# Four places for the split projections, the shared expert moved to the start, and the last stage's loads moved ahead, in a two-layer attention and expert kernel

## The chip, the cores and the metric

The kernel runs on one core of one Trainium2 chip. What counts is the device time of the whole program in microseconds (us), as the median of several runs. The core has five engines that run their own instruction lists and wait for each other by semaphores: PE (TensorE, matmul), DVE (VectorE), ACT (ScalarE), POOL (GpSimd) and SP (SyncE, which here only issues DMAs).

## What is computed

The input x has 4096 tokens of 128 features (2 sequences of 2048). Cut to what matters here, the reference is:

```
xn = layernorm(x)
s  = attention_block(xn)              # 8 heads on 64 features, and 8 heads on their Holt-smoothed copy
g  = silu(moe(xn))                    # 32 experts, 4 of them per token, plus a shared expert
x  = x + s * g
xn = layernorm(x); s = selective_scan_block(xn); g = silu(routed_mlp(xn)); x = x + s * g

# in moe:
scores = softmax(xn @ wg.T); keep the 4 best of 8 groups; top 4 experts; rank of each token in its expert
y = sum over the 4 experts of w * (silu(xe @ w1) * (xe @ w3)) @ w2
z = silu(xf @ sw1) * (xf @ sw3) @ sw2          # the shared expert, on all 4096 tokens
return y + z
```

## The kernel before

The order of all work is written out by hand, engine by engine; `wait_ge(sem, n)`, `after(engine, sem, n)` and, on SP, `hold(sem, n)` are the waits. Each engine's list runs in order, so a wait holds back all that stands behind it. Tokens are taken in `NB` = 8 blocks of 512. The program's stages are:

1. **Start.** Normalisation and its transpose `XNT` (L1514), routing logits (L1520), the Holt level (L1526 to L1534), with the attention input `XC`, which lies in the tile `YM`. `XC` is also stored to DRAM as `xct_d` (L473).
2. **Projections and routing.** For each block j PE makes Q and K (`qk`, L1564, two banks of PSUM, in turn 4, 5 and 6, 7) and V (`values`, L1572). Q and K go to DRAM as three bf16 parts each, whose sum is the float32 value: ACT writes the leading part (`lead`, L1166), DVE the remainder (`remainder`, L677), ACT the middle part (`middle`, L1172), POOL the last part (`part2`, L1432), and SP stores all six to `ql_d` and `kl_d` (L437). The parts of a block have one of two places, `part(parts, level, j % 2)`. DVE has the `remainder` calls written between the routing's top-4 search (L712 to L718), which ends in `sel_done` (L721). Then PE sums the selection over tokens (`ranks`, L1553 and L1554, in banks 0 to 3), and DVE makes each token's rank in its expert out of it (L730 to L752).
3. **Attention.** 16 units (8 groups of heads for 2 sequences). A unit's Q and K come back by 12 DMAs into `stacks` (L449, L451). DVE takes row maxima of the scores (`unit_max`, L758) out of PSUM banks 4 to 7, a unit ahead of the exponentials on ACT (L1202); PE does scores for the maxima (L1588), scores (L1633) and weighed values (L1606). In the second half of the units POOL scatters the tokens to their experts (L1472).
4. **Experts.** 32 experts, each a transpose, two products, a product back, and a store of the result to `oe_d` (L521).
5. **Shared expert.** PE (L1705, L1706), ACT (L1247), DVE (L804), PE (L1698), DVE (L797, into `YM`), over the 8 blocks, with the weights of "expert 32".
6. **Tail of layer 0 and projections of layer 1.** SP writes the softmax sums' reciprocals to DRAM (L525), loads the attention results of blocks 0 and 1 (`load_attn`, L533 to L535), and the constants of layer 1 (L554 to L556). DVE starts with a wait for all of these constants, then `normalise` (L830, L831), `attn_stats` (L813), `attn_apply` (L824 to L844), and `combine(j)` (L862), which adds to `YM` the four expert outputs of each token, gathered by POOL with 16 indirect DMAs to a block (L1497). The gathers start when all stores of L521 have landed.
7. **Selective scan and the last MLP** of layer 1.

## Time and profile before

| | us |
|---|---|
| median of 3 runs | 2137.68 (2133.76 to 2138.3) |
| the profiled execution, its time | 2140.73 |
| its span | 2138.9 |
| PE busy | 1884.9 |
| DVE busy | 1776.4 |
| ACT busy | 1444.4 |
| POOL busy | 344.0 |

The profile has one execution. PE is busy for 88% of the span and DVE for 83%, but both are averages over stages with different limits, so a change in one stage is read from that stage: which engine or DMA ends its waits.

### The profile page before, as it was taken

How to read it: one execution, taken by the hardware profiler on the slowest of the kernel's cores; microseconds unless marked ns; L12 is line 12 of the kernel's file. 1: busy time of each engine (PE TensorE's matmuls, PEld its weight loads, DVE VectorE, ACT ScalarE, POOL GpSimd, SP SyncE). 2: the span in 40 equal slices, each digit the busy share in tenths (PEclk: the TensorE clock that was granted, in tenths of full speed). 3: DMA queues.
4: the chain of work that ended last, by engine and by line, in shares of the span. 5: the costliest groups of instructions: out<-in, count | busy, mean ns of one | idle time of the engine just before them, and what ended most of it. 6: DMA issues, size and time to landing. Idle time of an engine off the chain costs nothing.

```text
span 2138.9 us, 33478 instructions
## 1 busy us (share of the span) xinstructions
PE 1884.9 (88%) x11734; PEld 719.9 (34%) x11734; DVE 1776.4 (83%) x2689; ACT 1444.4 (68%) x2807; POOL 344.0 (16%) x516
## 2 busy tenths in 40 slices
PE   7537999999999999999999999988997887599884
PEld 6201222222222222222222222216764444266563
DVE  6689999999999999999999999903347887478778
ACT  5204888888888888888888888883322344567542
POOL 1210000000000222222222222000027652000000
PEclk9656999999999999999999999999998889799896
DMA  3231121120010111111111111016754332321321
GB/s 84 83 116 44 46 71 65 47 84 26 25 35 24 40 46 36 46 42 35 51 38 38 49 37 49 8 32 178 205 162 123 108 112 73 101 71 54 101 76 30
DMA packets 145888, 144.01 MB, mean 67 GB/s; under 512 B 29451, under 2 KB 124687, under 8 KB 145572
## 3 DMA queue, kind: packets, MB, share of 16 engines
q1 hardware_dynamic: 137380, 124.71, 19.2%
q0 software_dynamic: 8352, 17.29, 2.7%
q8 instruction: 89, 1.46, 0.3%
q14 instruction: 67, 0.55, 0.1%
HBM read 81.06 MB, written 60.03 MB: 66 GB/s over the span
## 4 chain that ended last, share of the span: by engine, by line
PE 70%; DVE 14%; ACT 8%; issue 3%; DMA 2%; SPq 2%; POOL 1%; DVEq 0%; ACTq 0%
PE PS L1606 23%; PE PS L1633 18%; PE PS L1588 8%; DVE mxp L758 6%; PE PS L1680 3%; ACT probs L1202 3%; ACT SG L1187 2%; PE PS L1736 2%; PE PS L1836 2%; PE PS L1854 1%; PE PS L1667 1%; PE PS L1745 1%; PE PS L1857 1%; PE PS L1839 1%; DMA xs_d<-SG 1%
## 5 line engine op out<-in xcount | busy, mean ns | idle before, releaser
L758 DVE TENSOR_REDUCE mxp<-PS 128x1 f32<-128x1024 f32 x1024 | 1203.5, 1220 | 43.9 <-PE PS L1588 29.2
L1202 ACT ACTIVATE probs<-PS 128x512 f32<-128x512 f32 x2048 | 1061.7, 604 | 168.1 <-PE PS L1633 164.9
L1633 PE MATMUL PS<-stacks 51*128 51x512 bf16 x2048 | 615.8, 383 | 28.2 <-ACT probs L1202 16.8
L1588 PE MATMUL PS<-stacks 48*128 48x512 bf16 x2048 | 518.9, 393 | 49.1 <-DVE mxp L758 30.4
L1606 PE MATMUL PS<-probs,VH 128*32 128x512 f32 x4096 | 546.7, 606 | 6.8 <-ACT SG L1187 6.1
L1633 PEld LDWEIGHTS PS<-stacks 51*128 51x128 bf16 x2048 | 154.3, 94 | 681.1 <-ACT probs L1202 611.7
L1588 PEld LDWEIGHTS PS<-stacks 48*128 48x128 bf16 x2048 | 109.5, 94 | 217.0 <-DVE mxp L758 178.0
L1472 POOL DMA_INDIRECT xe_d<-xn_s,rows_s x128 | 126.0, 984 | 328.5 <-PE PS L1606 292.6
L1497 POOL DMA_INDIRECT VP<-oe_d,ROWI x128 | 133.4, 1042 | 255.7 <-DMA oe_d<-stacks 194.7
L771 DVE TENSOR_TENSOR stacks<-stacks,PS 128x640 f32<-128x640 f32 x32 | 26.2, 820 | 134.7 <-ACT stacks L1234 134.7
L1606 PEld LDWEIGHTS PS<-probs,VH 128*32 128x32 f32 x4096 | 81.6, 108 | 125.0 <-issue 109.2
L1450 POOL CAST spl<-nmx 128x16 bf16<-128x16 f32 x32 | 6.3, 196 | 562.8 <-DVE nmx L761 476.5
L1680 PE MATMUL PS<-stacks,ews 128*128 128x320 f32 x256 | 76.4, 441 | 5.9 <-DVE stacks L771 4.1
L1736 PE MATMUL PS<-wa,wff 128*128 128x512 f32 x64 | 47.1, 902 | 26.1 <-ACT wa L1257 26.1
L1234 ACT ACTIVATE stacks<-PS 128x640 f32<-128x640 f32 x32 | 22.5, 704 | 59.7 <-PE PS L1680 59.7
L1680 PEld LDWEIGHTS PS<-stacks,ews 128*128 128x128 f32 x256 | 46.1, 190 | 27.3 <-issue 9.0
L1191 ACT ACTIVATE mT<-PS 48x128 bf16<-48x128 bf16 x32 | 8.5, 267 | 67.2 <-PE PS L1594 67.2
L1458 POOL TENSOR_TENSOR VH<-VP,bvb 128x128 f32<-128x128 f32 x32 | 14.3, 451 | 202.1 <-PE PS L1606 202.1
L1260 ACT ACTIVATE probs<-PS,bcol 128x512 f32<-128x512 f32 x32 | 22.0, 687 | 31.4 <-PE PS L1736 31.4
L1225 ACT ACTIVATE stacks<-PS 128x640 f32<-128x640 f32 x32 | 22.5, 703 | 30.2 <-PE PS L1659 30.2
L1667 PEld LDWEIGHTS PS<-ews,stacks 128*128 128x128 f32 x320 | 40.7, 192 | 6.5 <-DVE stacks L771 1.6
L1564 PE MATMUL PS<-YM,wsq 128*128 128x512 f32 x32 | 24.7, 916 | 20.2 <-DVE wa L677 20.2
(344 smaller groups left out, 1922.4 us busy)
## 6 DMA issues: line engine op xcount, KB each, us to landing
xe_d<-zt SPq DMA_DIRECT2D x16, 640.0 KB
stacks<-xe_d SPq DMA_DIRECT2D x32, 320.0 KB, 3.3
oe_d<-stacks SPq DMA_DIRECT2D x32, 320.0 KB, 2.4
o_d<-SG SPq DMA_DIRECT2D x256, 32.0 KB, 1.6
ews<-in_ew_dram SPq DMA_DIRECT2D x33, 192.0 KB, 2.3
stacks<-ql_d SPq DMA_DIRECT2D x64, 96.0 KB
stacks<-kl_d SPq DMA_DIRECT2D x64, 96.0 KB
probs<-xs_d SPq DMA_DIRECT2D x18, 256.0 KB, 3.7
```

The source lines that it names most:

```text
L758: v.tensor_reduce(mxp[:, n // 2, n % 2:n % 2 + 1], MXB[n % 2].rearrange("p a c -> p (a c)"), X_AX, ALU.max).then_inc(mx_done, 1)
L1187: act.activation(OE[half][:, :], OB, ACT.Copy).then_inc(o_evac, 1)
L1202: act.activation(probs[:, at:at + 512], PS[:, bank_of(u, e), :], ACT.Exp, scale=float(1.0 / np.sqrt(np.float32(DK)))).then_inc(exp_done, 1)
L1472: pool.indirect_dma_start(xe_d, bass.IndirectOffsetOnAxis(rows_s[i][:, n:n + 1], 0), xn_s[i][:, :], None, bounds_check=E * CAP - 1, oob_is ...
L1497: pool.indirect_dma_start(GB[:, t % (2 * TB), n, :], None, oe_d, bass.IndirectOffsetOnAxis(ROWI[:, t, n:n + 1], 0), bounds_check=E * CAP, ...
L1588: mm = pe.matmul(MXB[n % 2][:, i, :], QS[w][o:o + MAXROWS, (n // 2) * P:(n // 2 + 1) * P], KS[w][o:o + MAXROWS, key:key + 512], start=True ...
L1606: mm = pe.matmul(OB[32 * jg:32 * jg + 32, :], VH[w][:, kt, :], probs[:, at:at + 512], start=(kt < 2), stop=(kt >= TCH - 2))
L1633: pe.matmul(PS[:, bank_of(u, e), :], KS[w][o:o + KROWS + 3, kt * P:(kt + 1) * P], QS[w][o:o + KROWS + 3, q0:q0 + 512], start=True, stop=Tr ...
L1667: mm = pe.matmul(o, hhe[w % 2][:, t * P:(t + 1) * P], EW[w][:, 2, :], start=True, stop=True)
L1680: mm = pe.matmul(PS[:, 2 + 2 * m + h, 0:CAP // 2], EW[w][:, m, :], xeT[w % 2][:, h * CAP // 2:(h + 1) * CAP // 2], start=True, stop=True)
L1736: pe.matmul(PS[:, 2 + f % 2, :], wff1[:, f * P:(f + 1) * P], f_(wa[3]), start=True, stop=True).then_inc(f_ready, 1)
L1836: pe.matmul(PS[:, b, :], BELOW, scaled[:, b, :], start=True, stop=True)
```

## The change

It has three parts.

- **Four places for the parts.** Blocks j % 4 of 0 and 1 keep the two places of before, blocks 2 and 3 get places in `stacks` (`QS[1]` to `QS[3]`, which are empty until the first unit loads). ACT's `lead(j)` waits for the store of block j-4 where it waited for that of block j-2.
- **The shared expert at the start.** It is taken out from behind the experts, on PE, ACT and DVE. Its weights are loaded behind x. On PE `shared_in(0)` stands ahead of `ranks`, the rest of it behind, ahead of the first scores for the maxima. ACT now takes the silu (into `SHG`) and also copies the other product out (`SHV`), POOL multiplies the two (`SHH`), and ACT copies the result to `YM`: DVE has no instruction of it. `SHG`, `SHV` and `SHH` lie in the tiles of the experts' weights, of `affine` and of `wff`, so the loads of `affine` and `wff` come later. `xct_d` is stored before the parts, since `YM` gets its result early. A `sem_inc(sums_read)` on DVE tells PE that banks 2 and 3 are read.
- **The tail's loads earlier.** `wff`, `affine` and all constants of layer 1 but `win` are loaded at the start of the attention; the reciprocal sums are stored at expert 8; `load_attn(0)` is issued at expert 30, ahead of the last two stores. Behind the last store come `load_attn(1)` and `win`.

```diff
@@ SP
+            load_weights(sp, E)
             for dst, src in CONSTS0:
...
-            sp.dma_start(affine[:, :, :], a["affine"].partition_broadcast(P)).then_inc(c_ld, 16)
             hold(ones_set, 5)
...
+            hold(h_out, TCH // TB)
+            hold(xc_ready, NB)
+            sp.dma_start(xct_d, XC).then_inc(xct_st, 16)
             for j in range(NB):
                 hold(part2, j + 1)
                 for parts, src, stored in ((ql_d, QPARTS, ql_st), (kl_d, KPARTS, kl_st)):
                     hold(stored, 48 * j)
                     for lv in range(3):
-                        sp.dma_start(parts[lv, :, j * 512:(j + 1) * 512], part(src, lv, j % 2)).then_inc(stored, 16)
+                        sp.dma_start(parts[lv, :, j * 512:(j + 1) * 512], part(src, lv, j % 4)).then_inc(stored, 16)
...
+            hold(c_ld, 16 * NCONST)
+            hold(sh_out, NB)
+            for dst, src in CONSTS_LATE:
+                sp.dma_start(dst, a[src]).then_inc(c_ld, 16)
+            sp.dma_start(affine[:, :, :], a["affine"].partition_broadcast(P)).then_inc(c_ld, 16)
+            sp.dma_start(alog[:, 0:2, :], a["alog"].partition_broadcast(P)).then_inc(c_ld, 16)
+            sp.dma_start(sc_aff[:, :, :], a["sc_aff"].partition_broadcast(P)).then_inc(c_ld, 16)
             repeat(sp, GROUPS // 4, lambda k: group(k, clear=True))
...
+                if e == 8:
+                    hold(at_sum, 1)
+                    for j in range(NB):
+                        sp.dma_start(rl_d[:, j * 512:(j + 1) * 512], LS[0][G * j:G * j + G, :]).then_inc(rl_st, 16)
+                if e == E - 2:
+                    hold(rl_st, 16 * NB)
+                    hold(xct_st, 16)
+                    hold(xt_ready, E)
+                    load_attn(0)
...
+            hold(hh_done, E)
             load_attn(1)
-            for dst, src in CONSTS1:
-                sp.dma_start(dst, a[src]).then_inc(c_ld, 16)
-            sp.dma_start(alog[:, 0:2, :], a["alog"].partition_broadcast(P)).then_inc(c_ld, 16)
-            sp.dma_start(sc_aff[:, :, :], a["sc_aff"].partition_broadcast(P)).then_inc(c_ld, 16)
+            hold(c_ld, 16 * NLATE)
+            sp.dma_start(win[:, :], a["win"]).then_inc(c_ld, 16)
@@ ACT
-                after(act, ql_st, 48 * (j - 1))
-                after(act, kl_st, 48 * (j - 1))
+                after(act, ql_st, 48 * (j - 3))
+                after(act, kl_st, 48 * (j - 3))
...
+            act.wait_ge(xct_st, 16)
+            for j in range(NB + 1):
+                if j < NB:
+                    act.wait_ge(sh_ready, j + 1)
+                    after(act, sh_product, j - 1)
+                    act.activation(SHG[j % 2], PS[:, 4 + 2 * (j % 2), :], ACT.Silu)
+                    act.activation(SHV[j % 2], PS[:, 5 + 2 * (j % 2), :], ACT.Copy).then_inc(sh_gated, 1)
+                if j > 0:
+                    act.wait_ge(sh_projected, j)
+                    act.activation(YM[:, TB * (j - 1):TB * j, :], PS[:, 2 + (j - 1) % 2, :].rearrange("p (t d) -> p t d", d=D), ACT.Copy).then_inc(sh_out, 1)
             write_rows(0, 1)
@@ POOL
+            for j in range(NB):
+                pool.wait_ge(sh_gated, j + 1)
+                after(pool, sh_projected, j - 1)
+                pool.tensor_tensor(SHH[j % 2], SHG[j % 2], SHV[j % 2], ALU.mult).then_inc(sh_product, 1)
@@ PE
+            def shared_in(j):
+                after(pe, sh_gated, j - 1)
+                for n in range(2):
+                    mm = pe.matmul(PS[:, 4 + 2 * (j % 2) + n, :], EW[0][:, n, :], XNT[:, j * 512:(j + 1) * 512], start=True, stop=True)
+                mm.then_inc(sh_ready, 1)
+
+            def shared_project(j):
+                pe.wait_ge(sh_product, j + 1)
+                after(pe, sh_out, j - 1)
+                for t in range(TB):
+                    mm = pe.matmul(PS[:, 2 + j % 2, t * P:(t + 1) * P], SHH[j % 2][:, t * P:(t + 1) * P], EW[0][:, 2, :], start=True, stop=True)
+                mm.then_inc(sh_projected, 1)
+
+            pe.wait_ge(ew_ld[0], 16)
+            pe.wait_ge(rest, NB - 1)
+            shared_in(0)
             pe.wait_ge(v_out, NB)
             ranks()
+            pe.wait_ge(rest, NB)
+            shared_in(1)
+            pe.wait_ge(sums_read, 1)
+            for j in range(NB):
+                shared_project(j)
+                if j + 2 < NB:
+                    shared_in(j + 2)
```

On PE, between the projections and the attention, there stood only the four products of `ranks`, and then the scores for the maxima:

```order
40 L1553 MATMUL PS<-probs,cst 128x512
41 L1554 MATMUL PS<-probs,onesq 128x512
42 L1553 MATMUL PS<-probs,cst 128x512
43 L1554 MATMUL PS<-probs,onesq 128x512
44 L1588 MATMUL PS<-stacks 128x512 x72
```

Now it is this (L1592 is `shared_in`, L1599 `shared_project`; four pairs of the same rows follow before the last two shown):

```order
40 L1592 MATMUL PS<-XNT,ews 128x512 x2
41 L1564 MATMUL PS<-probs,cst 128x512
42 L1565 MATMUL PS<-probs,onesq 128x512
43 L1564 MATMUL PS<-probs,cst 128x512
44 L1565 MATMUL PS<-probs,onesq 128x512
45 L1592 MATMUL PS<-XNT,ews 128x512 x2
46 L1599 MATMUL PS<-ews,wff 128x128 x4
47 L1592 MATMUL PS<-XNT,ews 128x512 x2
...
58 L1599 MATMUL PS<-ews,wff 128x128 x8
59 L1622 MATMUL PS<-stacks 128x512 x72
```

The scores for the maxima, 44 before and 59 now, have all eight blocks of the shared expert ahead of them.

On SP, behind the experts' last stores, there stood:

```order
473 L521 DMA oe_d<-stacks 128x5x128 x4
474 L525 DMA rl_d<-probs 16x512 x8
475 L533 DMA stacks<-o_d 128x1x512 x2
476 L534 DMA stacks<-rl_d 128x1x512
477 L535 DMA stacks<-xct_d 128x512
478 L533 DMA stacks<-o_d 128x1x512 x2
479 L534 DMA stacks<-rl_d 128x1x512
480 L535 DMA stacks<-xct_d 128x512
481 L554 DMA stacks<-in_win_dram 128x644
...
487 L556 DMA sc_aff<-in_sc_aff_dram 128x768
```

Now there stands (L535 to L537 is `load_attn`, L569 the experts' store):

```order
471 L569 DMA oe_d<-stacks 128x5x128 x3
472 L535 DMA stacks<-o_d 128x1x512 x2
473 L536 DMA stacks<-rl_d 128x1x512
474 L537 DMA stacks<-xct_d 128x512
475 L569 DMA oe_d<-stacks 128x5x128 x2
476 L535 DMA stacks<-o_d 128x1x512 x2
477 L536 DMA stacks<-rl_d 128x1x512
478 L537 DMA stacks<-xct_d 128x512
479 L574 DMA stacks<-in_win_dram 128x644
```

One `load_attn` has moved ahead of the last two stores, the stores of L525 have moved up to expert 8, and of the constants only `win` is left behind `load_attn(1)`.

## Rows read from the trace of the kernel before

**Rows 1.** Windows: us; busy PE, PEld, DVE, ACT, POOL; PE clock, DMA share, GB/s

```profile
98.00:111.00 13.00, 0.62 (x3) 0.33 (x2) 7.37 (x8) 5.20 (x10) 2.29 (x3) 0.63 0.22 74
...
300.00:600.00 300.00, 291.81 (x1972) 69.33 (x1964) 289.20 (x252) 260.74 (x513) 9.42 (x36) 1.00 0.16 51
...
1585.00:1607.00 22.00, 21.41 (x99) 13.28 (x97) 10.60 (x17) 6.06 (x9) 13.05 (x14) 1.00 0.77 206
```

**Rows 2.** The chain of waits, one round of the projections: start, us, what

```profile
99.48 0.69 ACT HH L1166
...
106.47 2.01 DMA kl_d<-wa
108.59 0.69 ACT HH L1166
```

**Rows 3.** Groups of DVE, 61.5 to 107.2 us: busy, mean ns, idle before

```profile
L677 DVE SCALAR_TENSOR_TENSOR wa<-PS,bcol,HH 128x512 f32<-128x512 f32 x5 | 3.8, 751 | 17.5 <-ACT SG L1166 17.5
...
L713 DVE TENSOR_TENSOR probs<-probs,WK 128x1024 bf16<-128x1024 f32 x2 | 3.6, 1804 | 0.1
```

**Rows 4.** Timeline of DVE: start, us, instruction, idle before it

```profile
55.30 2.06 DVE L718 SCALAR_TENSOR_TENSOR probs<-probs 128x1024 f32<-128x1024 bf16 x1
...
59.97 1.23 DVE L713 TENSOR_TENSOR probs<-probs,WK 128x1024 bf16<-128x1024 f32 x1
...
106.50 0.69 DVE L721 TENSOR_SCALAR probs<-probs 128x1024 f32<-128x1024 f32 x1
...
117.37 1.22 DVE L730 COPY probs<-PS 128x1024 f32<-128x1024 f32 x1 [3.98 <-PE PS L1554]
...
139.84 36.29 DVE L758 TENSOR_REDUCE mxp<-PS 128x1 f32<-128x1024 f32 x32
```

**Rows 5.** Timeline of POOL in the projections

```profile
54.15 2.13 POOL L1432 TENSOR_TENSOR SG<-wa,HH 128x512 bf16<-128x512 f32 x1 [25.44 <-ACT wa L1172]
...
101.86 1.15 POOL L1432 TENSOR_TENSOR SG<-wa,HH 128x512 bf16<-128x512 f32 x1 [6.96 <-ACT wa L1172]
```

**Rows 6.** Timeline of PE, projections to the first maxima

```profile
48.21 1.88 PE L1564 MATMUL PS<-YM,wsq 128*128 128x512 f32 x4
...
93.16 3.75 PE L1564 MATMUL PS<-YM,wsq 128*128 128x512 f32 x4 [4.09 <-DVE wa L677]
96.71 1.92 PE L1572 MATMUL PS<-wsq,YM 128*128 128x128 f32 x8
111.43 2.07 PE L1553 MATMUL PS<-probs,cst 128*128 128x512 f32 x2 [12.81 <-ACT VP L1180]
...
135.94 1.04 PE L1588 MATMUL PS<-stacks 48*128 48x512 bf16 x4 [18.67 <-DMA stacks<-kl_d]
```

**Rows 7.** Timeline of PE, one block of the shared expert

```profile
1593.83 1.05 PE L1698 MATMUL PS<-ews,HH 128*128 128x128 f32 x8
...
1596.44 1.05 PE L1698 MATMUL PS<-ews,HH 128*128 128x128 f32 x8
```

**Rows 8.** The chain of waits, experts to tail

```profile
1600.30 7.42 DMA sc_aff<-in_sc_aff_dram
1607.74 0.70 DVE stacks L830
```

**Rows 9.** Timeline of SP: first load of unit 0; L525's stores behind the experts

```profile
121.72 0.80 SPq L449 DMA_DIRECT2D stacks<-ql_d  x1
...
1586.60 3.82 SPq L525 DMA_DIRECT2D rl_d<-probs  x8
```

**Rows 10.** Timeline of POOL and DVE: gathers of two blocks, and their use

```profile
1589.99 1.05 POOL L1497 DMA_INDIRECT VP<-oe_d,ROWI  x1 [194.67 <-DMA oe_d<-stacks]
...
1630.98 1.14 POOL L1497 DMA_INDIRECT VP<-oe_d,ROWI  x1 [0.30 <-issue]
...
1627.75 4.66 DVE L862 SCALAR_TENSOR_TENSOR YM<-VP,WK,YM 128x128 f32<-128x128 f32 x16
...
1649.10 4.66 DVE L862 SCALAR_TENSOR_TENSOR YM<-VP,WK,YM 128x128 f32<-128x128 f32 x16
```

More of the change, by code:

```diff
@@ L287, in build @@
         ones_set = sem("ones_set")
-        x_ld = [sem(f"x_ld{i}") for i in range(NB // 2)]
+        xz_ld = [sem(f"xz_ld{i}") for i in range(4)]
         var_ready, std_ready = sem("var_ready"), sem("std_ready")
@@ L339, in build @@
                              "g_st"))
-        z_ld, fw_ld = [sem(f"z_ld{i}") for i in range(4)], sem("fw_ld")
+        fw_ld = sem("fw_ld")
+        sh_ready, sh_gated, sh_product, sh_projected, sh_out, sums_read = (
+            sem(n) for n in ("sh_ready", "sh_gated", "sh_product", "sh_projected", "sh_out", "sums_read"))
         yl_ready, pr_ready, s2_done = (
@@ L367, in build @@
                                               wa[0].rearrange("p t c -> p (t c)"), wa[3].rearrange("p t c -> p (t c)"))]
+        ews_flat = ews.rearrange("p e m c -> p (e m c)")
+        aff_flat = affine.rearrange("p i c -> p (i c)")
+        SHG = [ews_flat[:, 3 * P + i * 512:3 * P + (i + 1) * 512] for i in range(2)]
+        SHV = [aff_flat[:, i * 512:(i + 1) * 512] for i in range(2)]
+        SHH = [wff[:, i * 512:(i + 1) * 512] for i in range(2)]
         QPARTS, KPARTS = halves16[0:3], halves16[3:6]
@@ L467, in load_max @@
                     sp.dma_start(QS[w][o + KROWS:o + KROWS + 3, :], mT[:, :]).then_inc(m_ld[w], 16)
-            hold(h_out, TCH // TB)
-            hold(xc_ready, NB)
-            sp.dma_start(xct_d, XC).then_inc(xct_st, 16)
             load_max(0, 0)
@@ L623, in _ @@
                 for i in range(GP):
-                    hold(z_ld[i], 32 * s)
+                    hold(xz_ld[i], 32 * s + 16)
                     if s >= 2:
@@ L676, in remainder @@
                 for n, (left, parts) in enumerate(((QREST, QPARTS), (KREST, KPARTS))):
-                    ins = v.scalar_tensor_tensor(left[w], PS[:, 4 + 2 * w + n, :], bcol[:, n:n + 1], part(parts, 0, w), ALU.add, ALU.subtract)
+                    ins = v.scalar_tensor_tensor(left[w], PS[:, 4 + 2 * w + n, :], bcol[:, n:n + 1], part(parts, 0, j % 4), ALU.add, ALU.subtract)
                 ins.then_inc(rest, 1)
@@ L790, in _ @@
             expert_out(E - 1, 3, E // 2 - 1)
-            def shared_out(j, w):
-                v.wait_ge(mo_ready, E + j + 1)
-                if isinstance(j, int) and j == 0:
-                    v.wait_ge(xct_st, 16)
-                v.tensor_copy(YM[:, bass.ds(TB * j, TB), :], PS[:, 4 + w, :].rearrange("p (t d) -> p t d", d=D)).then_inc(ym_done, 1)
-            def shared(k):
-                for w in range(2):
-                    j = 2 * k + w
-                    v.wait_ge(sg_done, E + j + 1)
-                    after(v, mo_ready, E + j - 1)
-                    v.tensor_tensor(HH[w][:, :], SG[w][:, :], PS[:, 2 + w, :], ALU.mult).then_inc(hh_done, 1)
-                    if not (w == 0 and isinstance(k, int)):
-                        shared_out(j - 1, 1 - w)
-            repeat(v, NB // 2, shared)
-            shared_out(NB - 1, 1)
+            v.wait_ge(c_ld, 16 * NLATE)
             def stats(src, groups, bn, agg):
@@ L1171, in middle @@
                 for left, parts in ((QREST, QPARTS), (KREST, KPARTS)):
-                    ins = act.activation(part(parts, 1, j % 2), left[j % 2], ACT.Copy)
+                    ins = act.activation(part(parts, 1, j % 4), left[j % 2], ACT.Copy)
                 ins.then_inc(part1, 1)
@@ L1241, in _ @@
                 act.wait_ge(oe_st[half], 64 * UNITS)
-            def shared(k):
-                for w in range(2):
-                    act.wait_ge(mh_ready, E + 2 * k + w + 1)
-                    act.wait_ge(hh_done, E + 2 * k + w - 1)
-                    act.activation(SG[w][:, :], PS[:, w, :], ACT.Silu).then_inc(sg_done, 1)
-            repeat(act, NB // 2, shared)
             def root(what, agg, groups):
@@ L1691, in _ @@
             pe.wait_ge(hh_done, E)
-            pe.wait_ge(ew_ld[0], 16 * (E // 4) + 16)
-            def shared_project(j, w):
-                pe.wait_ge(hh_done, E + j + 1)
-                after(pe, ym_done, j - 1)
-                for t in range(TB):
-                    mm = pe.matmul(PS[:, 4 + w, t * P:(t + 1) * P], HH[w][:, t * P:(t + 1) * P], EW[0][:, 2, :], start=True, stop=True)
-                mm.then_inc(mo_ready, 1)
-            def shared(k):
-                for w in range(2):
-                    j = 2 * k + w
-                    pe.wait_ge(hh_done, E + j - 1)
-                    pe.matmul(PS[:, w, :], EW[0][:, 0, :], XNT[:, bass.ds(j * 512, 512)], start=True, stop=True)
-                    pe.matmul(PS[:, 2 + w, :], EW[0][:, 1, :], XNT[:, bass.ds(j * 512, 512)], start=True, stop=True).then_inc(mh_ready, 1)
-                    if not (w == 0 and isinstance(k, int)):
-                        shared_project(j - 1, 1 - w)
-            repeat(pe, NB // 2, shared)
-            shared_project(NB - 1, 1)
+            pe.wait_ge(oe_out, E)
+            pe.wait_ge(c_ld, 16 * NLATE)
             cols = lambda t: slice(t * P, (t + 1) * P)
```

68 lines of the change are left out of this document (33 added, 35 removed).

## The prediction

> **What bounds the kernel now.** I read the windows first [rows 1]. In the attention TensorE is at its full clock (1.00) and busy for 291.81 of 300 us, DVE for 289.20: nothing of the change is in that stage but nine loads on SP, so I take its length as it is. What is left are two places where several engines wait. From 98 to 111 us DVE is busy for 7.37 of 13 us and PE for 0.62. From 1585 to 1607 us PE is busy for 21.41 of 22 us, and all of that is the shared expert.
>
> In the first place the chain of waits shows why [rows 2]. ACT's leading part of one block starts at 99.48, that of the next at 108.59. Between them lie the other parts, six issues on SP and 2.01 us until the last store has landed. That is a round of 9.11 us for a block, and its last link is a DMA: a place must be stored before it is written again. DVE, which has the routing in the same list, stands still for it: 17.5 us in five waits ahead of L677 up to the end of the top-4 search [rows 3]. `sel_done` comes at 106.50 + 0.69 = 107.2 [rows 4], PE starts `ranks` at 111.43, since the last V copy ends only then [rows 6], and DVE goes on at 117.37. It needs 139.84 - 117.37 = 22.5 us to its first maximum [rows 4]. Unit 0's loads have landed at 135.94 [rows 6], so it is DVE's list that ends last here.
>
> In the second place the reader is to look at what DVE waits for at 1607.74: not the shared expert, but 7.42 us for the landing of `sc_aff`, the last of the tail's loads [rows 8]. The two end within a microsecond of each other. To take out either alone would bring next to nothing; the change takes out both.
>
> **The change, first part: the start.** All instants are those of the profiled execution.
>
> *Selection.* With four places ACT waits for the store of four blocks ago. DVE's own work is (106.50 - 59.97 - 17.5) = 29 us for a bit over five blocks, some 5.2 us a block, so that store has 20 us to land where the round takes 9. The 17.5 us go. PE does not take their place for long: one block's Q, K and V take 3.75 + 1.92 us in a row at the low clock [rows 6], 5.7 against DVE's 5.2, but the first of them 1.88 at the high one, and PE that has no pauses gets its clock back (the shared expert's window has 1.00, with the same kind of products, and the projections' end 0.63 [rows 1]).
>
> Something comes back. L713 takes 1.23 us alone and 1.80 where POOL works beside it [rows 3, 4]; L718 took 2.06, while POOL's own operation took 2.13 where it otherwise takes 1.15 [rows 4, 5]. An elementwise DVE operation on two SBUF tiles and a POOL one do not run at once; the second waits. Before, this cost DVE 0.57 us in five blocks (two are the x2 of L713). When ACT no longer waits, POOL's pair follows the remainder at once and meets L717/L718 or L713 each time, as at 54.15: I take 2.06 - 1.23 = 0.83 for seven blocks, less the 2.9 of before, so about +2.6 (with the cost left as it was it would be 0). `sel_done`: 107.2 - 17.5 + 2.6 = 92.3.
>
> The Trainium skill ("SBUF — State Buffer", section "Who interferes with whom") says the same of this port: whoever issues first has the shared pair for the whole instruction and the other blocks, for DVE operations with two SBUF inputs against GpSimd's reads. By that rule the products that the change gives to POOL are not free though POOL is idle; without it the start would come out 5.5 + 2.6 = 8 us better. The trace agrees (2.13 against 1.15).
>
> *Ranks.* V of block 7 is now copied before the selection ends, as its ACT operation no longer stands behind a store; so the 111.43 - 107.2 = 4.2 us go too. `shared_in(0)` fits ahead: its wait (the seventh remainder) ends some 8 us before `sel_done`, it takes at most 3.75. `ranks` to DVE's copy takes 117.37 - 111.43 = 5.9 again: 98.3, which is 19 us earlier than before.
>
> *DVE to the first maximum.* 98.3 + 22.5 = 120.8. Seven of POOL's eight products fall in here. A POOL operation of 1.15 us can hold DVE up by nothing (when it meets a reduction, one half of L741 to L742) or by up to 1.1; I take 0.8, so 5.5, and 126.3.
>
> *PE to the first maximum.* Behind `ranks` stands `shared_in(1)`, at the low clock 3.75 [rows 6]: 102. Then eight rounds of `shared_project` and `shared_in`. PE's own work of a round is 1596.44 - 1593.83 = 2.61 us at the full clock [rows 7]. But the round is also a chain: two ACT operations of 0.6 to 0.69, one POOL product of 1.15 to 2.13 [rows 5], handovers of 0.1 each, so 2.7 to 3.8. I take 3.3, since DVE's elementwise work is dense here: 102 + 7 x 3.3 + 1.05 = 126.2. Both lists meet at 126.4. The other conditions are earlier. The last parts are stored by 103 (last remainder at 94, ACT 1.2, POOL 2.3 to 4.2, store 4.5), and unit 0's loads take 135.94 - 121.72 = 14.2 [rows 6, 9]: 117. If this cover of 9 us were gone, each us late would count in full. The early store of `xct_d` runs between 47 and 58 us, ahead of the first part's store at 58, the late loads cost SP some 5 us while it has nothing due for the first unit; both at nothing.
>
> **First part: 139.84 - 126.4 = 13.4 us.** Bounds: the DVE waits at 1.1 each, a round of 3.8 and a slow clock for two blocks give 132.5, a gain of 7; no added DVE wait and rounds of 2.7 give 119.3, a gain of 20.5. I take the middle because the nearest rows (2.06, 2.13) are those of dense DVE work.
>
> **Second part: the end of the experts.** The shared expert's 21.5 us on PE, 16 DVE and 8 ACT operations go. SP's list then decides when DVE may start. `load_attn(1)` is issued at 1586.60, where L525 began [rows 9], and `win` behind it. By the shapes in the list of SP's DMAs these are 4 x 262 and 330 KB, and four gathers of 64 KB each run beside them: 1.6 MB. At the 206 GB/s of the window [rows 1] that is 7.8 us: 1594.4, and with a last handover I take 1595. DVE starts 1607.74 - 1595 = 12.7 us earlier, not 21.5.
>
> Next late are the gathers. They wait for the stores alone, so they start at 1590 as before [rows 10], and 32 of them, two blocks, are issued by 1630.98 + 1.14 = 1632.1 [rows 10]; with 2 us to land that is 1614 for block 0 and 1634 for block 1. Block 0's were used at 1627.75 and block 1's at 1649.10. Shifted by 12.7 they are wanted at 1615 and 1636.4: just covered, by 1 and 2 us. And PE, which came from the shared expert at its full clock, now has 10 idle us ahead of `residual(0)`. I put 1.3 us for the lower clock there. **Second part: 12.7 - 1.3 = 11.4 us.** Bounds: `load_attn(0)` ahead of the last two stores makes these land 2 to 3 us later and the gathers with them, 8.5; if `win` lands at 1593 the gathers' 15 us (1649.10 - 1634) is the ceiling.
>
> **Sum.** 13.4 + 11.4 = 24.8 us. The span of 2138.9 becomes 2114; the profiled time of 2140.73 is 3 us above the median of 2137.68, so the median becomes 2113.
>
> **The rivals.**
>
> *The moved work costs little at the start.* POOL's products meet reductions and PE keeps the full clock; a gain of 20 there, 2106 in all. For it: rows 7's round of 2.61. Against it: 2.13 in rows 5. 0.17.
>
> *The shared expert becomes the bound of the start.* PE stays at the low clock, where a round takes 3.75 + 1.92 = 5.7 us: 102 + 8 x 5.7 = 147, and the first part loses 8 us instead of gaining 13; 2134. A half of it (rounds of 4.3) gives 133 and 2119. For it: 0.63 in the window around this place [rows 1]. Against it: PE has no pause then. The full case 0.03, the half 0.16.
>
> The Trainium skill ("TensorE: Matmul & The Clock Gate", section "What's actually happening") says that the clock is at one of two levels and rises after sustained work. By that the full case can't last; that rule speaks against this rival, and 1.00 in the shared expert's window agrees.
>
> *The gathers or the loads hold the tail.* They come 6 us late in blocks 0 and 1: second part 5, 2119. For it: a cover of only 1 to 2 us. 0.12.
>
> *Slower.* The attention takes more. Its 1250 us are PE's at the clock of 1.00 [rows 1]. If PE, which now works on through the start, were granted 2% less in it, 25 us would be lost; that is the point from which the change loses. Nothing in the trace shows 0.98 there. 0.03.
>
> *The change doesn't do what it says:* the four places bring nothing since SP's own issues (six of 0.45 and a landing of 2, with one store held until the last has landed) make the round. That would be 2.7 + 2.0 = 4.7 us, below DVE's 5.2; it would take a few us off the gain of this one part; only if the experts' end brought nothing either would the time be that of before. 0.02, which I count as no change together with the full case of the low clock.
>
> **How the numbers follow.** My forecast, the sum within 5 us, has 0.47. 2113 is its value, its own range 2108 to 2118. It is at 2103 and 2124 that no more than 2 in 10 is left out: the unchanged and slower cases, and the outer ends of the bounds. A measurement can tell about 0.2% here, 4 us. Within it: 0.03 + 0.02 = 0.05. Slower: 0.03. Faster by more, the rest: 0.92.
>
> **What would show it.** In the profile after: no wait for a store ahead of ACT's leading part; `sel_done` near 92; the copy behind `ranks` near 98; elementwise DVE operations of 1.8 to 2.3 us beside POOL's products; PE's rounds near 3.3 us; the first maximum near 126 us. At the end, DVE's first instruction of the tail some 9 us behind the last expert's copy, released by `win`; the first `combine` within 2 us of its gathers; experts and attention as long as before. Wrong would be: the first maximum before 120 or after 132, a wait of more than 3 us for gathers at `combine(0)` or `combine(1)`, or another attention length.

## The result, and the profile after

The median went from 2137.99 us (14 runs, 2133.76 to 2141.37) to 2112.24 us (14 runs, 2109.53 to 2132.11, all but one below 2113.5): a ratio of 0.9884, 95% interval 0.9867 to 0.99, where 2113 was forecast. The profiled execution of the changed kernel took 2112.58 us, with a span of 2110.8. All ratios here are of fast runs alone, so one slow run of the loads-only kernel below (2389.07 us, clock 0.715) is not in its ratio.

One correction: the text on the kernel before speaks of 16 units of the attention; there are 32 (16 groups of heads for 2 sequences). No number rests on it.

Windows of the changed kernel, columns as in [rows 1]:

```profile
98.00:111.00 13.00, 12.54 (x52) 6.94 (x51) 10.72 (x12) 5.92 (x11) 5.96 (x5) 0.96 0.31 104
300.00:600.00 300.00, 291.66 (x1965) 69.35 (x1968) 289.39 (x254) 261.06 (x513) 9.79 (x39) 1.00 0.16 51
1572.00:1581.00 9.00, 0.00 (x0) 0.00 (x0) 0.71 (x3) 0.00 (x0) 3.54 (x4) 0.58 0.79 251
```

The 13 us in which PE had 0.62 us of work now have 12.54, and the 300 us of attention are as they were (291.66 against 291.81). Behind the experts nine us are left in which PE and ACT do nothing and the DMAs move 251 GB/s.

DVE's timeline (start, us, instruction, idle before it and what ended it). It answers to [rows 3, 4] up to 125.42, then to [rows 8, 10]:

```profile
61.32 1.53 DVE L732 TENSOR_TENSOR probs<-probs,iob 128x1024 bf16<-128x1024 bf16 x1
...
91.45 1.52 DVE L739 TENSOR_SCALAR probs<-probs 128x1024 f32<-128x1024 f32 x1
...
99.79 1.23 DVE L748 COPY probs<-PS 128x1024 f32<-128x1024 f32 x1 [4.38 <-PE PS L1565]
...
102.83 2.11 DVE L754 TENSOR_TENSOR probs<-probs 128x960 f32<-128x960 f32 x1
...
105.23 2.19 DVE L754 TENSOR_TENSOR probs<-probs 128x896 f32<-128x896 f32 x1
...
108.78 1.38 DVE L753 COPY probs<-probs 128x512 f32<-128x512 f32 x1
...
125.42 1.22 DVE L777 TENSOR_REDUCE mxp<-PS 128x1 f32<-128x1024 f32 x1
...
1572.07 0.28 DVE L796 COPY stacks<-PS 128x128 f32<-128x128 f32 x1
1580.64 0.69 DVE L834 TENSOR_TENSOR stacks<-stacks 128x512 f32<-128x512 f32 x1 [8.29 <-DMA stacks<-in_win_dram]
...
1587.68 1.15 DVE L817 BATCH_NORM_STATS2 bnh<-PS 128x6 f32<-128x64 f32 x8 [4.30 <-PE PS L1741]
...
1591.34 0.20 DVE L826 RECIPROCAL mvh<-mvh 128x8 f32<-128x8 f32 x1 [1.64 <-ACT mvh L1260]
...
1602.97 4.67 DVE L866 SCALAR_TENSOR_TENSOR YM<-VP,WK,YM 128x128 f32<-128x128 f32 x16
...
1623.31 4.66 DVE L866 SCALAR_TENSOR_TENSOR YM<-VP,WK,YM 128x128 f32<-128x128 f32 x16 [1.12 <-DMA VP<-oe_d,ROWI]
```

The search ends at 91.45 + 1.52 = 92.97, and no wait stands ahead of L695 (L677 before) any more. The first maximum starts at 125.42, 14.4 us earlier than in [rows 4]. The last expert's copy (L796) is at 1572.07, the tail's first instruction 8.57 us behind it, and the first `combine` at 1602.97, 24.8 us earlier than in [rows 10].

This execution was a little late at the start. Four of the kernels below have the same start as this one (loads late, `win` early, and both runs with the root); in them the copy (L748) comes at 98.59 to 98.66 and the first maximum at 124.23 to 124.29, so 1.2 us of the 125.42 are a difference between executions. The stretch from the copy to the first maximum is the same in all five, 25.6 us.

PE's timeline, answering to [rows 6]:

```profile
93.12 2.04 PE L1564 MATMUL PS<-probs,cst 128*128 128x512 f32 x2 [4.08 <-DVE probs L739]
...
96.66 1.91 PE L1564 MATMUL PS<-probs,cst 128*128 128x512 f32 x2
...
99.52 1.88 PE L1592 MATMUL PS<-XNT,ews 128*128 128x512 f32 x4
101.24 1.05 PE L1599 MATMUL PS<-ews,wff 128*128 128x128 f32 x8
...
121.20 1.16 PE L1599 MATMUL PS<-ews,wff 128*128 128x128 f32 x8 [1.62 <-POOL wff L1444]
122.29 0.60 PE L1622 MATMUL PS<-stacks 48*128 48x512 bf16 x4
126.70 0.61 PE L1622 MATMUL PS<-stacks 48*128 48x512 bf16 x2 [3.80 <-DVE mxp L777]
```

From the first `shared_project` (101.24) to the eighth (121.20) there are seven rounds of 2.85 us. The first scores start at 122.29, and PE then waits 3.80 us for DVE: PE's list ends 3 us ahead of DVE's.

POOL's timeline, two of the products, answering to [rows 5]; the last row is the first gather:

```profile
97.95 1.26 POOL L1444 TENSOR_TENSOR wff<-ews,affine 128x512 f32<-128x512 f32 x1
...
108.06 1.82 POOL L1444 TENSOR_TENSOR wff<-ews,affine 128x512 f32<-128x512 f32 x1 [1.58 <-ACT affine L1227]
...
1576.54 1.06 POOL L1508 DMA_INDIRECT VP<-oe_d,ROWI  x1 [194.96 <-DMA oe_d<-stacks]
```

SP's timeline, answering to [rows 9]; and the chain of waits at the end of the experts and ahead of `combine(1)`:

```profile
102.40 0.79 SPq L463 DMA_DIRECT2D stacks<-ql_d  x1
...
1566.29 1.33 SPq L535 DMA_DIRECT2D stacks<-o_d  x2
...
1569.95 2.78 SPq L569 DMA_DIRECT2D oe_d<-stacks  x2
1572.78 1.20 SPq L535 DMA_DIRECT2D stacks<-o_d  x2
...
1575.30 0.43 SPq L574 DMA_DIRECT2D stacks<-in_win_dram  x1
```

```profile
1572.38 3.19 DMA oe_d<-stacks
...
1617.83 5.46 DMA VP<-oe_d,ROWI
```

The 5.46 us run from the start of the gather's issue at 1617.83 to its landing; POOL is busy with the issue for the first 1.22 of them.

ACT has one row that the prediction did not speak of:

```profile
1589.81 1.28 ACT L1260 ACT_TABLE_LOAD   x1 [21.53 <-DVE mvh L822]
```

It loads the table for the square root behind the wait for DVE, and DVE waits for the root (1.64 us at L826). In the kernel before the same load lay at 1605.16, directly behind the shared expert's last silu, and DVE's wait was 0.28 us. The experiments bear out that the place of the shared expert makes the difference: 0.28 us with the loads moved alone, 1.64 with the loads late. Why ACT loads the table ahead of its wait in the one list and behind it in the other, no row shows.

### The profile page after: what moved, and what is told of

Same layout as the page of the kernel before. It is cut to its first block, busy times and chain, and to the rows that moved or that the text cites. A ratio compares the mean times of both kernels' runs of the same rounds, so it can differ in the third digit from the quotient of the medians.

```text
span 2110.8 us, 33428 instructions
## 1 busy us (share of the span) xinstructions
PE 1879.0 (89%) x11734; PEld 717.2 (34%) x11734; DVE 1770.7 (84%) x2673; ACT 1456.2 (69%) x2825; POOL 366.0 (17%) x524
## 4 chain that ended last, share of the span: by engine, by line
PE 71%; DVE 15%; ACT 7%; issue 4%; DMA 2%; POOL 1%; SPq 1%; DVEq 0%; POOLq 0%; ACTq 0%
PE PS L1640 23%; PE PS L1668 18%; PE PS L1622 8%; DVE mxp L777 6%; PE PS L1715 3%; ACT probs L1206 3%; ACT SG L1191 2%; PE PS L1853 2%; PE PS L1871 2%; PE PS L1754 1%; PE PS L1702 1%; POOL VP L1508 1%; DMA xs_d<-SG 1%; PE PS L1763 1%; PE PS L1874 1%
## 5 line engine op out<-in xcount | busy, mean ns | idle before, releaser
L1754 PE MATMUL PS<-wa,wff 128*128 128x512 f32 x64 | 41.2, 795 | 26.2 <-ACT wa L1264 26.2
L1248 ACT ACTIVATE stacks<-PS 128x640 f32<-128x640 f32 x32 | 22.5, 704 | 59.7 <-PE PS L1715 59.7
L1239 ACT ACTIVATE stacks<-PS 128x640 f32<-128x640 f32 x32 | 22.5, 703 | 30.1 <-PE PS L1694 30.1
L1702 PE MATMUL PS<-ews,stacks 128*128 128x128 f32 x320 | 41.0, 275 | 1.4 <-DVE stacks L796 1.4
L1853 PE MATMUL PS<-VP,cst 128*128 128x512 f32 x64 | 35.2, 676 | 7.0 <-DVE VP L951 7.0
L1191 ACT ACTIVATE SG<-PS 128x512 f32<-128x512 f32 x64 | 38.0, 594 | 4.6 <-PE PS L1640 1.2
```

Source lines behind the costliest of these rows:

```text
L1191: act.activation(OE[half][:, :], OB, ACT.Copy).then_inc(o_evac, 1)
L1702: mm = pe.matmul(o, hhe[w % 2][:, t * P:(t + 1) * P], EW[w][:, 2, :], start=True, stop=True)
L1754: pe.matmul(PS[:, 2 + f % 2, :], wff1[:, f * P:(f + 1) * P], f_(wa[3]), start=True, stop=True).then_inc(f_ready, 1)
L1853: pe.matmul(PS[:, b, :], BELOW, scaled[:, b, :], start=True, stop=True)
```

## The experiments

My theory was that of the prediction. At the start DVE stands still for stores that wait for a place, and the price of the moved work is POOL holding DVE up. At the end two things finish nearly together, and each edit pays only with its partner. The rivals were that one of the edits alone brings the gain, that POOL's work costs nothing, and later that something else (the gathers) already bounds the tail.

**Two places instead of four.**

```diff
-part(..., j % 4)                       # on SP, DVE, ACT, POOL
-after(act, ql_st, 48 * (j - 3))
+part(..., j % 2)
+after(act, ql_st, 48 * (j - 1))        # and kl_st
```

> The changed kernel with two places for the parts, as before; shared expert and loads stay moved. My theory (the wait for a place is what DVE stood still for): the round of 9.1 us is back, the selection ends near 107 us and not at 93, the copy behind the ranks starts near 117, the first maximum near 143 (22.5 us and 3 for POOL's products), so 17 to 18 us later than the 125.4 of the changed kernel; time 2129 to 2131. Rival (the places bring nothing, the shared expert's place or the early store of xct_d made the gain): first maximum at 125 to 128, time 2112 to 2115.

Measured: 2131.07 us, ratio 0.9971 (0.996 to 0.9982). DVE's timeline of this kernel:

```profile
100.90 0.75 DVE L695 SCALAR_TENSOR_TENSOR wa<-PS,bcol,HH 128x512 f32<-128x512 f32 x1 [4.12 <-ACT SG L1170]
...
117.09 1.22 DVE L748 COPY probs<-PS 128x1024 f32<-128x1024 f32 x1 [3.64 <-PE PS L1565]
...
142.71 3.48 DVE L777 TENSOR_REDUCE mxp<-PS 128x1 f32<-128x1024 f32 x3
```

The waits for stores are back, 17.4 us in five of them, and the copy is where it was before (117.37 in [rows 4]). The first maximum is now 2.9 us later than before: with the shared expert moved but not the places, the start pays for POOL's products and gets nothing back. Of the 25.7 us, 18.8 rest on the four places (2131.07 - 2112.24). What is left, 6.9 (6.4 against the kernel before as it ran beside this one, 2137.46), is the tail's gain less what the start loses; in the trace `combine(0)` comes 7.5 us earlier than before (1620.22 against 1627.75). The other half of this pair, four places with the shared expert left behind the experts, was not run: so that the places would pay at the start without a partner is what the rows suggest, not what a run shows.

**The tail's loads where they were** (`affine` and `wff` stay early, since the shared expert needs their tiles).

```diff
-if e == 8: ... rl_d stores;  if e == E - 2: ... load_attn(0)
-CONSTS_LATE, alog and sc_aff ahead of the attention
+all of these behind the last expert's store, as before
```

> The changed kernel with the tail's loads where they were before (the reciprocal sums' stores, both load_attn and the constants of layer 1 behind the last expert's store; wff and affine stay early). My theory (both had to go): DVE's first instruction of the tail starts some 21.5 us behind the last store's issue, not 8, so near 1594 and not at 1580.6, combine(0) near 1614, no wait for gathers; time 2122 to 2125, all of the second part lost. Rival (the shared expert's 21.5 us on PE were the wait): time within 2 us of the changed kernel's 2112.

Measured: 2123.69 us, ratio 0.994 (0.9917 to 0.9962). DVE's timeline:

```profile
1570.33 0.28 DVE L795 COPY stacks<-PS 128x128 f32<-128x128 f32 x1
1592.18 0.69 DVE L833 TENSOR_TENSOR stacks<-stacks 128x512 f32<-128x512 f32 x1 [21.57 <-DMA sc_aff<-in_sc_aff_dram]
```

DVE starts 21.85 us behind the last expert, exactly as before (1607.74 - 1585.89): with the shared expert gone and the loads late, nothing is gained at this place. The 13.8 us that are left against the kernel before as it ran beside this one (2137.46) come from the start: the first maximum is 15.6 us earlier (124.24), the last expert's copy too.

**The loads early, and nothing else** (the kernel before with them).

```diff
+CONSTS1 without win, alog, sc_aff ahead of the attention; rl_d stores at expert 8
+load_attn(0) at expert 30; load_attn(1) and win behind the last store
```

> The kernel before with the tail's loads alone moved early (win behind load_attn(1)); two places, shared expert behind the experts. My theory: the tail starts when the shared expert's last copy ends, 0.0 to 0.7 us earlier than the 1607.74 of before; time 2136 to 2138, no change. Rival (the loads were the wait alone): time 2125, 12 us faster.

Measured: 2139.41 us, ratio 1.0 (0.9986 to 1.0013), 1.4 us above the range that I expected. The shared expert's last copy is at 1608.89, and the tail starts at 1609.50, in the same place as before (21.8 us behind the last expert). The two runs together show the pair: loads alone nothing, shared expert alone nothing at this place, both 13.3 us. One row more is of use below:

```profile
1616.67 1.15 DVE L819 BATCH_NORM_STATS2 bnh<-PS 128x6 f32<-128x64 f32 x8 [4.43 <-PE PS L1729]
```

From the tail's start to this row it is 7.17 us, where the kernel before has 6.01 (1607.74 to 1613.75), although PE had just finished the shared expert at a granted clock of 1.00 and waited 2.20 us, as before (2.23). The clock from 1608 to 1616 is 0.70.

**No product on POOL.** PE takes the silu alone as the shared expert's second input; the multiplication by the other product is left out.

```diff
-pool.tensor_tensor(SHH[j % 2], SHG[j % 2], SHV[j % 2], ALU.mult)
-pe.wait_ge(sh_product, j + 1)
+pe.wait_ge(sh_gated, j + 1)             # and SHG where SHH was
```

ACT's silu of block j then waits for the last product of block j-2 instead of POOL's.

> The changed kernel with POOL's eight products of the shared expert left out: the last product of it takes the silu alone, so the shared expert's output is another. My theory (POOL's product and an elementwise DVE operation on two SBUF tiles exclude each other): DVE's list from the copy behind the ranks to the first maximum takes 22.5 us again, where the changed kernel has 125.42 - 99.79 = 25.6; PE's list ends near 118; the first maximum is near 122.3, time 2109. Rival (the 3.1 us are from the loads of the units or from PSUM's readers): 25.6 us stay, time 2112.

Measured: 2109.24 us, ratio 0.9873 (0.9851 to 0.9895). DVE's timeline:

```profile
100.00 1.23 DVE L748 COPY probs<-PS 128x1024 f32<-128x1024 f32 x1 [4.41 <-PE PS L1561]
...
103.04 1.16 DVE L754 TENSOR_TENSOR probs<-probs 128x960 f32<-128x960 f32 x1
...
106.94 0.43 DVE L753 COPY probs<-probs 128x512 f32<-128x512 f32 x1
...
122.58 4.61 DVE L777 TENSOR_REDUCE mxp<-PS 128x1 f32<-128x1024 f32 x4
```

Copy to first maximum takes 22.58 us, as before (22.5), against 25.63 in the changed kernel. The difference of 3.05 us is three instructions: 2.11 against 1.16, 2.19 against 1.09, 1.38 against 0.43. PE's rounds take 2.61 us, and its first scores start at 119.54 (expected near 118). So POOL's products cost 3.1 us, not nothing and not 5.5. One of the three, the copy at 108.78, reads a single tile: not only operations on two SBUF tiles are held up.

**`win` in a tile of its own, loaded with the other constants.**

```diff
-win = stack_f[:, 4096:4096 + NIN]       # loaded behind load_attn(1)
+win = sb("win", [P, NIN])               # loaded ahead of the attention
```

> The changed kernel with win in a tile of its own, loaded with the other constants at the start of the attention. In the changed kernel DVE waits 8.3 us for it behind the last expert. My theory (the gathers are next, they start with the last store's landing at 1576.5 and POOL issues them at 1.30 us each): DVE starts at once, near 1573 to 1575, combine(0) waits for its gathers until 1599 to 1602, combine(1) stays at 1622 to 1623.3; time 0 to 1.5 us less, 2111. Rival (the tail is as early as its first instruction): combine(1) near 1616, time 2104 to 2105.

Measured: 2110.67 us, ratio 0.9865 (0.9848 to 0.9881). DVE's timeline:

```profile
98.66 1.22 DVE L746 COPY probs<-PS 128x1024 f32<-128x1024 f32 x1 [3.18 <-PE PS L1563]
...
1572.46 0.69 DVE L832 TENSOR_TENSOR stacks<-stacks 128x512 f32<-128x512 f32 x1 [1.09 <-DMA stacks<-xct_d]
...
1579.77 0.69 DVE L832 TENSOR_TENSOR stacks<-stacks 128x512 f32<-128x512 f32 x1 [5.89 <-DMA stacks<-xct_d]
...
1599.07 4.69 DVE L864 SCALAR_TENSOR_TENSOR YM<-VP,WK,YM 128x128 f32<-128x128 f32 x16 [2.53 <-DMA VP<-oe_d,ROWI]
...
1619.91 4.66 DVE L864 SCALAR_TENSOR_TENSOR YM<-VP,WK,YM 128x128 f32<-128x128 f32 x16 [2.58 <-DMA VP<-oe_d,ROWI]
```

The wait of 8.29 us for `win` is gone, and in its place stand 5.89 for `load_attn(1)`'s last load and two waits for gathers. `combine(1)` starts 48.8 us behind the last expert (1571.09), against 51.2 in the changed kernel: of 8.3 us, 2.4 arrive. I had expected `combine(1)` at 1622 to 1623.3, the rival near 1616; it came at 1619.91. The gathers are the next bound.

**The sums over all tokens first.** `ranks` computes banks 2 and 3, which DVE's copy needs, ahead of banks 0 and 1.

```diff
+for bank, weights in ((2, onesq), (0, cst[:, P + 2:2 * P + 2])):
+    for h in range(2): mm = pe.matmul(PS[:, bank + h, :], weights, sel(h), ...)
+    mm.then_inc(lg_ready, 1)            # DVE waits for 2, and for 3 ahead of L757
```

> The changed kernel with the ranks' two products for banks 2 and 3 ahead of the two for banks 0 and 1, each pair with a signal of its own; DVE copies banks 2 and 3 first in any case. My theory (DVE's list bounds the start): the copy starts near 96.9 and not at 99.79, PE's list is as before and ends near 122.3, the first maximum is near 122.6; time 2.5 to 3 us less, 2109.5. Rival (PE's list and the shared expert's chain bound the start): first maximum at 125, time 2112.

Measured: 2110.46 us, ratio 0.9869 (0.985 to 0.9887). DVE's timeline:

```profile
96.81 1.23 DVE L748 COPY probs<-PS 128x1024 f32<-128x1024 f32 x1 [1.39 <-PE PS L1566]
...
123.91 22.70 DVE L778 TENSOR_REDUCE mxp<-PS 128x1 f32<-128x1024 f32 x20
```

DVE's copy came 3 us earlier than in the changed kernel's profile, and the first maximum 1.5 us (expected 122.6). Against the four executions with the same start as the changed kernel it is 1.8 and 0.3 us. The stretch between is 27.1 us long instead of 25.63, 4.6 over the 22.5 without products: all eight products now lie in it, where the first used to fall into DVE's wait, and they meet other instructions. So what POOL's products cost depends on which DVE instructions they fall beside. PE had finished its list at 120.78 and was not the bound.

**Both of these.** The edits of the last two kernels together.

> Both of the above, the version that may beat the changed kernel: 2.5 to 4.5 us less than it, 2108 to 2109.5, if the two places add up. Rival for the sum: what the start gives is lost again, 2112.

Measured: 2109.8 us, ratio 0.9863 (0.9847 to 0.988), just above the range that I expected; span 2105.7. First maximum at 122.46, 26.1 us behind the copy, with the same lists at the start as the kernel just before; then waits for gathers of 5.10 us at `combine(0)` and 2.91 at `combine(1)`. The intervals of the last three ratios all overlap that of the changed kernel (0.9867 to 0.99); only the places in the traces separate them.

**POOL's last part set instead of subtracted.** The last parts of Q and K are zero in this kernel.

```diff
-ins = pool.tensor_tensor(part(parts, 2, j % 4), left[j % 2], part(parts, 1, j % 4), ALU.subtract)
+ins = pool.memset(part(parts, 2, j % 4), 0.0)
```

> The changed kernel with POOL's subtractions for the last parts replaced by a memset of the same 512 elements to zero, so the last parts are zero; POOL still has two operations to a block, but they read nothing. In the changed kernel DVE's elementwise operations take 1.53 and 2.06 us in every block where they take 0.69 and 1.23 alone, some 0.83 us for each block. My theory, with the rule of the Trainium skill (SBUF - State Buffer, Who interferes with whom: two SBUF inputs against a GpSimd operation that reads SBUF): all of this goes, the selection ends near 87 and not at 92.97, and the POOL operations are no longer than some 0.6 us; the first maximum near 119.5, time 2106. Rival (any POOL operation excludes DVE's, or the time is lost for another reason): selection at 90 to 93, time 2109 to 2112.

This kernel and the next ran on a chip where the kernel before took 2231.84 us, with waits in the tail that the other traces don't have, so their times (here 2180.95, ratio 0.9772, 0.9741 to 0.9803) are not set against the others and only places are read. DVE's timeline, then POOL's:

```profile
78.79 1.23 DVE L731 TENSOR_TENSOR probs<-probs,WK 128x1024 bf16<-128x1024 f32 x1
80.05 0.69 DVE L732 TENSOR_TENSOR probs<-probs,iob 128x1024 bf16<-128x1024 bf16 x1
84.61 1.22 DVE L736 SCALAR_TENSOR_TENSOR probs<-probs 128x1024 f32<-128x1024 bf16 x1
```

```profile
79.34 0.52 POOL L1439 MEMSET wa<- 128x512 bf16 x1
```

L732 takes 0.69 us where it took 1.53 and L736 1.22 where it took 2.06 in all three rounds, and L739 0.69 where it took 1.52; the search ends at 86.56 instead of 92.97 (expected near 87). That the memsets do lie beside DVE's work, L731 shows: it takes 1.23 us, as alone, with the memset of 79.34 inside it. So here a POOL instruction that writes a tile but reads none did not hold DVE up; the subtraction, which reads two, does, for 0.83 us a meeting. The Trainium skill ("SBUF — State Buffer", section "Who interferes with whom") says that a DVE instruction with two SBUF inputs contends with a GpSimd instruction that reads SBUF and not with one that only writes it. The trace agrees (1.23 us for L731). The first maximum came at 117.46 (expected 119.5), as the four products of `ranks` took only 3.7 us here; the stretch from the copy to it is 27.0 us.

**A square root ahead of time.** ACT takes a root of a constant behind its last expert, so that the table is loaded where ACT has nothing to do. It was run twice, since the first run fell on the chip just named (2191.95 us; the wait for the root was 0.36 us, and waits of 14.86 us ahead of `combine(0)` and 4.10 within it, such as only the traces of that chip have, hid the rest: it decides nothing).

```diff
+act.activation(hn[:, 0:1], ident[:, 0:1], ACT.Sqrt)
```

> The changed kernel with one small square root on ACT behind the last expert, so that ACT's table load of 1.28 us lies in the wait for the tail's loads and not behind DVE's first variances. My theory: DVE's wait for the first root falls from 1.64 to 0.3 us, combine(0) comes 1.3 us earlier against the last expert's copy (near 29.5 us behind it, not 30.9), and combine(1) waits longer for its gathers and stays 51.2 us behind the copy (49.5 to 51.5): time unchanged within 0.5 us, 2112. Rival (the gathers are no bound, 1.12 us was chance): combine(1) moves too, 1.3 us less.

> The dummy square root on ACT behind its last expert again, on another chip. Both theories agree that the table load leaves DVE's wait for the root (1.64 us in the changed kernel's trace, some 0.4 now). My theory: the root is on the path between DVE's start of the tail (8.3 to 8.7 us behind the last expert's copy) and combine(0), so combine(0) comes 1.3 us earlier behind the last copy than the 30.90 us of the changed kernel (1572.07 to 1602.97), some 29.6. Rival: the gathers of block 0, 26 us behind the last copy in the other runs, or PE at its lower clock take it up, and combine(0) stays within 0.3 us of 30.9. The median would be 2111 by the one and 2112 by the other, which a comparison can hardly tell; the places in the trace do.

Measured in the second run: 2111.28 us, ratio 0.9883 (0.9866 to 0.99). DVE's timeline:

```profile
1579.72 0.69 DVE L834 TENSOR_TENSOR stacks<-stacks 128x512 f32<-128x512 f32 x1 [9.55 <-DMA stacks<-in_win_dram]
...
1589.46 0.20 DVE L826 RECIPROCAL mvh<-mvh 128x8 f32<-128x8 f32 x1 [0.36 <-ACT mvh L1261]
...
1601.02 4.70 DVE L866 SCALAR_TENSOR_TENSOR YM<-VP,WK,YM 128x128 f32<-128x128 f32 x16
```

From DVE's start of the tail to `combine(0)` it is 21.30 us, against 22.33 in the changed kernel: the load was on the path, and 1.0 of its 1.28 us come back. `combine(1)` comes 52.2 us behind the last expert (1622.05), against 51.2. But `win` landed 1.3 us later in this run, so that behind the last expert (1569.89) `combine(0)` came at 31.1 us, which is the rival's number of 30.9, not mine of 29.6. By the number I was wrong: I had taken the landing of `win` as fixed, and it moves by as much as the whole edit brings.

**All three edits** (`win`'s tile, the sums first, the root).

> win in a tile of its own and the sums over all tokens first, both as before, with the dummy square root besides. Combine(0) of the run with both waited 5.10 us for its gathers, combine(1) 2.91. My theory: the gathers are the bound there, so the 1.3 us of the root only lengthen these waits (to about 6.4 at combine(0)), and combine(1) stays 50 us behind the last copy, as 1617.58 - 1567.47 = 50.1 there; the median stays near 2110. Rival: DVE's list is still the bound at combine(1), which then comes at 48.8 us or earlier, and the median goes to 2108.5.

Measured: 2107.51 us (2107.2 to 2109.59), ratio 0.9861 (0.9842 to 0.988), the lowest median of all. DVE's timeline:

```profile
1596.75 4.67 DVE L865 SCALAR_TENSOR_TENSOR YM<-VP,WK,YM 128x128 f32<-128x128 f32 x16 [5.43 <-DMA VP<-oe_d,ROWI]
...
1618.16 4.66 DVE L865 SCALAR_TENSOR_TENSOR YM<-VP,WK,YM 128x128 f32<-128x128 f32 x16 [3.19 <-DMA VP<-oe_d,ROWI]
```

`combine(1)` comes 50.3 us behind the last expert's copy (1567.88), as in the run without the root (50.1), and not at 48.8: the gathers are the bound there. The root's 1.28 us do not all reach the wait for them, which is 5.43 us and not 6.4: `load_attn(1)` landed 0.6 us later in this run and DVE waited 0.50 for the next block's load. The median is below the 2110 that I expected and nearer to the rival's 2108.5, but the spans (2105.6 and 2105.7) are alike, so I read no gain of the root out of it.

## Why the prediction was right

The time came out within 1 us of the forecast, and both mechanisms with it. Several terms of the sum were mis-sized, in both directions, so that the total is as close as this is in part luck.

*Selection* (forecast 92.3, measured 92.97). The 17.5 us of waits went, all of them. POOL's last parts met DVE once in each block as forecast: seven instructions from 61.32 to 91.45 are longer by 0.83 us, 5.8 in all, less the 2.9 of before. That leaves 2.9, where the prediction's own 7 x 0.83 - 2.9 was written as 2.6; the end is 3.3 us behind 107.2 - 17.5 = 89.7. The condition was too narrow: L739 (1.52 against 0.69 us) reads one tile and is held up too, as is the copy L753 further on.

*Ranks* (98.3, measured 99.79, and 98.6 in the four other executions with this start). Besides the 0.7 us of the selection, the four products take 6.6 us instead of 5.9 in the profiled execution, at a granted clock of 0.54. With `win` early the same products take 5.4 at 0.68, behind the same wait of 4.08 us, and in the kernel before 5.9 behind 12.81. So the clock sets their length, but the wait ahead of them does not say what it will be; the miss is one of this execution.

*DVE to the first maximum* (28 us, measured 25.63). The mis-sized term is "I take 0.8, so 5.5" for POOL's products: they cost 3.1. Three of seven hold an elementwise instruction up by a microsecond each. Of the others, two come second to a DVE operation and wait themselves (1.74 us at 114.01, 1.65 at 116.62), one lies beside a copy out of PSUM that takes 1.22 us as alone, and one costs 0.05. The price of one meeting (1.1 at most) was right, the number of meetings that DVE pays for too high.

*PE to the first maximum* (126.2, measured 122.29). `shared_in(1)` takes 1.88 us and not 3.75, since the clock had risen during `ranks` (the granted clock from 98 to 111 is 0.96), and the rounds take 2.85 us and not 3.3. The two lists did not meet: PE was 3 us ahead. Had PE's term been right, PE's list would have ended last (126.2 against 125.42). The lower bound of 119.3 does not follow from its own terms: DVE's list without added waits is 120.8, and PE's with rounds of 2.7 ends at 102 + 7 x 2.7 + 1.05 = 122. First part in all: 14.4 instead of 13.4 us at the first maximum (15.6 in the other executions), of which 13.8 are left at the last expert's copy (1585.89 before, 1572.07 after). The unit's loads start at 102.40 (forecast 103) and stay hidden.

*The end of the experts.* DVE starts 13.3 us earlier behind the last expert, for a forecast of 12.7, released by `win` as forecast. From DVE's start to L817 it is 7.04 us where it was 6.01, which is 1.03 us for the 1.3 put for the clock, and PE's first products there (1582.20) come behind 10.78 idle us at a granted clock of 0.57 (1582 to 1588). That the idle time brings the low clock is not shown: with the loads moved alone PE waited 2.20 us and the same stretch took 7.17. The table load of 1.28 us was in no term; with the shared expert behind the experts it lay in ACT's idle time, and moving it uncovered the load. DVE's wait for the root went from 0.28 to 1.64 us. This second part gave 11.0 us at `combine(0)` (24.8 - 13.8) for a forecast of 11.4, so two small misses cancelled. At `combine(1)` it is 12.0 in spite of the wait for gathers, since between the two PE's eight products on `wff` took 3.89 us where they took 5.68 before.

*Gathers.* The cover of 1 us at `combine(0)` held; the one of 2 us at `combine(1)` did not, by 1.12 us. The last gather of block 1 landed 51.2 us behind the last expert's copy, where 48.1 were put (1634 - 1585.89). Of these 3.1 us, 2.2 are the landing, which took 4.2 us behind the end of its issue (1619.05 to 1623.29) and not 2; POOL began 0.4 later and took 0.4 longer for the 32 issues.

*Open:* the shift is 25.8 us at `combine(1)` and `combine(2)`, then between 24.4 and 27.0 up to the last `combine` (1805.70 before, 1778.73 after), and 28.1 at the end of the span. These last 2.3 us are in neither term and have no cause in the program that I know. The medians are 25.75 apart: the profiled execution of the kernel before lay 2.7 us above its median and that of the changed kernel 0.3, which is as much as the difference.

The rivals: the half case of the shared expert as a bound and the held tail did not come; "little cost" named the right direction (3.1 of 5.5 us) but not the 20 us. The attention's clock stayed at 1.00.

## What to carry to other kernels

Where two waits end within a microsecond of each other, price the two edits only as a pair: here the loads alone and the moved work alone were both worth nothing at the tail, and together 13.3 us. Before work is moved away from a place, ask what it covered there: here a table load of 1.28 us. When a wait is taken out, name the next one by its distance; behind 8.3 us for `win` stood 5.89 for `load_attn(1)` and then the gathers, and only 2.4 us could be had. Before a term is called wrong by a microsecond, look at the same place in the other traces: here the ranks' copy came 1.2 us earlier in four of them.

## What was not expected of the hardware

- The cost of the same eight POOL products beside the same DVE list was 3.1 us in the changed kernel, with two places and with late loads, 3.6 with both small edits, and 4.6 with the sums first, though the last two have the same lists at the start: it depends on the alignment to within a microsecond.
- The same four products of `ranks` behind the same wait of 4.08 us took 6.6 us in one execution (granted clock 0.54) and 5.4 in another (0.68).
- Operations that read one tile were held up by POOL as well: a TENSOR_SCALAR of 128x1024 took 1.52 us for 0.69, a copy of 128x512 1.38 for 0.43.
- A `memset` of 128x512 on POOL took 0.5 us and held up no DVE instruction, where the subtraction took 2.13 beside DVE and 1.15 alone.
- The landing of a gather beside the loads of `load_attn` took 5.46 us from the start of its issue, where the median of the 48 gathers up to 1640 us is 2.7.
- One chip ran the kernel before in 2231.84 us where the others took 2137 to 2139, with the attention's window the same in the trace of the kernel with the last part set (PE 291.54 us busy, clock 1.00) and waits in the tail that the traces of the other chips don't have (13.47 us there, 14.86 with the root).
